# Attention values of a Flamingo-style block: split-precision matmuls into one strip, or plain float32 matmuls into four column quadrants

## The chip, the core and the metric
The kernel runs on one core of one Trainium2 chip. The metric is the time of the whole program on the device in microseconds (us). The kernel before takes 1038.49 us (median of 3 runs, 1037.32 to 1039.15).

## The reference
The program computes two residual blocks over x of shape (4, 512, 512): four batches of 512 tokens with 512 features.

```python
x = x + tanh(g_xattn) * mixture(layernorm(x), token_ids, W, W, W)   # one of 4 experts per token
x = x + tanh(g_ffn)   * ffn(layernorm(x), ...)

def ffn(hidden, ...):                      # H = 16 heads, HD = 32, R = 16, F = 2048
    x = rmsnorm(hidden, ln1_w)
    q, k, v = x @ Wq.T, x @ Wk.T, x @ Wv.T               # each split into 16 heads
    scores = q @ k.T / sqrt(32), masked below the diagonal (causal)
    attn = softmax(scores) @ v, heads joined, @ Wo.T
    mod = 0.1 * tanh(attn @ A)                           # A is (512, 16)
    h = rmsnorm(hidden, ln2_w)
    gate = silu(h @ W_in.T + mod * (h @ A) @ B)
    return hidden + (gate * (h @ W_up.T)) @ W_down.T
```

Only `attn @ A`, 16 numbers a token, is wanted of the attention. The kernel therefore folds Wo and A into the values ahead of time: each head has values of 512 keys by 16, and the sum over all heads of probabilities times values is `attn @ A`.

## The kernel before, in words
A first stage works on 19 items of tokens sorted by expert; then each of the four batches has an attention stage and an MLP stage of 16 chunks. The engines run programs that are written out by hand and meet at semaphores; each engine works strictly in its own order. Nearly all products are "split": each float32 operand is held as a high part and a rest, both in the type float32r, and a product is three matmuls (high*high, rest*high, high*rest).

The attention stage of a batch takes the 16 heads one after the other in `head_step`. For one head there are four engines in a ring:

- TensorE multiplies queries by keys into banks 0, 1 and 2 (`score_rows`, line 700): four matmuls, of 512, 384, 128 and 256 columns, since causal rows need only the keys ahead of them (1280 score columns in all for 512 queries).
- VectorE (`maxima`, line 1405) adds the mask, copies the scores to SBUF and keeps each row's maximum. ScalarE (`exponentials`, line 1038) takes the exponentials and their row sums. VectorE inverts the sums (line 1411, semaphore `rr_ok`). The rows are then multiplied by the inverse: the 512-wide part on VectorE (line 1415), the 128-wide part on ScalarE (line 1045), the 256- and 384-wide parts on GpSimd (line 493).
- TensorE turns the probabilities (ten 128x128 transposes, line 734) into banks 6, 5 and 4, which hold 256, 512 and 512 columns.
- ScalarE copies each of the three banks as the high part (line 953), VectorE subtracts it from the bank to get the rest (`low`, line 1391; semaphore `pt_lo`).
- TensorE attends (`attend`, line 797): the values of a head, also split, lie side by side as [high | rest | high of the neighbour], 48 columns, and are the stationary operand; the high and the rest of the turned probabilities are the moving one. That is eight float32r matmuls of 512, 512, 384, 384, 256, 256, 128 and 128 columns, all of them into rows 0 to 47 of bank 7, which gathers all heads. GpSimd splits the values of four heads at a time (`values_of`, lines 503 and 505).

TensorE's order in the step of head n is: turn head n+1, middle scores of n+3, attend head n with the last scores of n+3 between, first scores of n+4, and then a "filling" that belongs to something else: half a query or key projection for a later group of heads (`project_part`, steps 0 to 6), a quarter of the first MLP chunk's up product (`up_part`, line 851, steps 9 to 12), or half of the low-rank product (`low_rank_part`, line 768, steps 13 and 14). GpSimd also splits the projection weights (lines 428 and 432) after heads 0, 2 and 4.

When the last head is attended, a short chain makes the modulation: copy rows 32 to 47 of bank 7 (ScalarE), add rows 0 to 15 (VectorE, line 1544), tanh (ScalarE), two products and a split (`z_ok`, `zs_ok`). TensorE meanwhile runs the first chunk's gate product and the second chunk's up product, 12 matmuls of 512 columns each, and then waits for `zs_ok` in `modulate` (line 839).

Scores and maxima of head n may be written only when head n-3 has been turned (three buffers, `NP = 3`).

## Time and profile before

| | us |
|---|---|
| median of 3 runs | 1038.49 |
| the profiled execution, time | 1034.66 |
| its span, first to last instruction | 1032.9 |
| TensorE matmul busy | 1005.7 (97%) |
| VectorE busy | 702.4 (68%) |
| ScalarE busy | 603.7 (58%) |
| GpSimd busy | 279.2 (27%) |

The busy shares are averages over three kinds of stage. In the first batch the attention runs from about 178 us (first turned probabilities) to 243.6 us; in it VectorE, ScalarE and TensorE are all close to full, while in the MLP stages TensorE alone is. The granted TensorE clock is 1.00 of full speed in every stretch that was asked for.

### The profile page before, as it was taken

How to read it: one execution, taken by the hardware profiler on the slowest of the kernel's cores; microseconds unless marked ns; L12 is line 12 of the kernel's file. 1: busy time of each engine (PE TensorE's matmuls, PEld its weight loads, DVE VectorE, ACT ScalarE, POOL GpSimd, SP SyncE). 2: the span in 40 equal slices, each digit the busy share in tenths (PEclk: the TensorE clock that was granted, in tenths of full speed). 3: DMA queues.
4: the chain of work that ended last, by engine and by line, in shares of the span. 5: the costliest groups of instructions: out<-in, count | busy, mean ns of one | idle time of the engine just before them, and what ended most of it. 6: DMA issues, size and time to landing. Idle time of an engine off the chain costs nothing.

```text
span 1032.9 us, 16779 instructions
## 1 busy us (share of the span) xinstructions
PE 1005.7 (97%) x5140; PEld 830.0 (80%) x5141; DVE 702.4 (68%) x1841; ACT 603.7 (58%) x1447; POOL 279.2 (27%) x276
## 2 busy tenths in 40 slices
PE   6999999999999999999999999999999999999998
PEld 5787888777888888778888888778888887888886
DVE  7866755996665559985665489966655599754443
ACT  4564456997444448985344379963444499843332
POOL 4536124861000117640000148600001187300000
PEclk9999999999999999999999999999999999999999
DMA  6635133344222416434332354343234254222221
GB/s 231 216 141 173 41 122 93 83 93 163 93 91 91 132 54 184 95 104 153 96 92 91 112 158 94 77 165 96 94 98 148 57 159 100 85 82 91 91 91 52
DMA packets 47073, 115.78 MB, mean 112 GB/s; under 512 B 6800, under 2 KB 6800, under 8 KB 46096
## 3 DMA queue, kind: packets, MB, share of 16 engines
q1 hardware_dynamic: 43968, 105.06, 34.1%
q0 software_dynamic: 3040, 9.96, 2.8%
q8 instruction: 28, 0.46, 0.2%
q14 instruction: 37, 0.30, 0.1%
HBM read 76.46 MB, written 13.37 MB: 87 GB/s over the span
## 4 chain that ended last, share of the span: by engine, by line
PE 87%; DVE 4%; POOL 3%; DMA 3%; issue 2%; ACT 1%; SPq 1%; DVEq 0%
PE bank L537 67%; PE bank L734 6%; PE bank L797 6%; PE bank L700 3%; DMA stack<-wr 2%; POOL big L493 2%; PE bank L839 1%; PE bank L851 1%; DVE big L1405 1%; PE bank L593 1%; PE bank L768 1%; PE bank L608 1%; PE bank L651 1%; SPq L321 1%; DVE wr L1391 0%
## 5 line engine op out<-in xcount | busy, mean ns | idle before, releaser
L537 PE MATMUL bank<-hT,wr 128*128 128x512 f32 x1488 | 358.0, 390 | 0.0
L537 PEld LDWEIGHTS bank<-hT,wr 128*128 128x128 f32 x1488 | 279.2, 188 | 60.7 <-issue 1.6
L537 PE MATMUL bank<-wr,actr 128*128 128x512 f32 (+1 forms) x1224 | 301.6, 396 | 2.3 <-DVE actr L1373 1.5
L537 PEld LDWEIGHTS bank<-wr,actr 128*128 128x128 f32 x1224 | 227.8, 189 | 50.4 <-issue 3.0
L493 POOL TENSOR_SCALAR big<-big,rr 128x256 f32<-128x256 f32 (+1 forms) x124 | 149.2, 1212 | 76.1 <-DVE rr L1411 75.7
L432 POOL TENSOR_TENSOR wqs<-wstage,wqs 128x512 fp32r<-128x512 f32 x32 | 43.3, 1362 | 436.3 <-ACT wqs L953 435.0
L1436 DVE SCALAR_TENSOR_TENSOR wr<-stream,lns,wr 128x256 fp32r<-128x256 f32 x256 | 121.7, 536 | 52.2 <-ACT wr L1065 52.2
L1038 ACT ACTIVATE big<-big,nb 128x512 f32<-128x512 f32 (+3 forms) x256 | 140.6, 560 | 9.3 <-DVE nb L1405 9.3
L1391 DVE TENSOR_TENSOR wr<-bank,wr 128x512 fp32r<-128x512 f32 (+1 forms) x224 | 125.7, 607 | 19.3 <-ACT wr L953 18.6
L953 ACT ACTIVATE wr<-bank 128x512 fp32r<-128x512 f32 (+1 forms) x224 | 110.3, 529 | 33.5 <-PE bank L537 20.8
L953 ACT ACTIVATE actr<-act_sb 128x512 fp32r<-128x512 f32 x64 | 40.4, 632 | 146.0 <-DVE act_sb L1450 146.0
L1077 ACT ACTIVATE sil<-bank 128x512 f32<-128x512 f32 x64 | 38.2, 596 | 136.1 <-PE bank L839 136.1
L1405 DVE CUSTOM_DVE_ANT_0 big<-bank,masks 128x512 f32<-128x512 f32 (+3 forms) x256 | 110.1, 485 | 3.6 <-PE bank L700 3.5
L1065 ACT ACTIVATE wr<-stream,lns 128x256 fp32r<-128x256 f32 x256 | 108.4, 495 | 0.0
L734 PE MATMUL bank<-ident,big 128*128 128x128 f32 x640 | 88.7, 278 | 8.0 <-POOL big L493 5.1
L537 PE MATMUL bank<-hT,wqs 128*128 128x512 f32 x384 | 95.9, 393 | 0.0
L734 PEld LDWEIGHTS bank<-ident,big 128*128 128x128 f32 x640 | 70.9, 140 | 30.2 <-issue 15.9
L1391 DVE TENSOR_TENSOR wr<-stream,wr 128x512 fp32r<-128x512 f32 x64 | 43.8, 689 | 71.8 <-ACT wr L953 71.7
L797 PE MATMUL bank<-wr 128*48 128x256 f32 (+3 forms) x512 | 92.1, 310 | 0.0
L537 PEld LDWEIGHTS bank<-hT,wqs 128*128 128x128 f32 x384 | 71.5, 188 | 15.0
L1450 DVE TENSOR_TENSOR act_sb<-bank,sil 128x512 f32<-128x512 f32 x64 | 44.2, 691 | 56.9 <-PE bank L537 51.4
L1391 DVE TENSOR_TENSOR actr<-act_sb,actr 128x512 fp32r<-128x512 f32 x64 | 44.3, 692 | 44.7 <-ACT actr L953 44.7
(174 smaller groups left out, 990.3 us busy)
## 6 DMA issues: line engine op xcount, KB each, us to landing
stream<-in_wmlp SPq DMA_DIRECT2D x64, 512.0 KB, 4.0
stack<-wr SPq DMA_DIRECT2D x192, 128.0 KB, 2.3
stream<-in_wmlp SPq DMA_DIRECT2D x64, 256.0 KB, 2.7
big<-in_x SPq DMA_DIRECT2D x4, 1024.0 KB
big<-y_rows SPq DMA_DIRECT2D x4, 1024.0 KB, 5.6
residual<-big SPq DMA_DIRECT2D x4, 1024.0 KB
big<-residual SPq DMA_DIRECT2D x4, 1024.0 KB, 6.5
out<-big SPq DMA_DIRECT2D x3, 1024.0 KB, 4.8
```

The costliest lines, as they stand in the source:

```text
L432: g.tensor_tensor(wqs[:, LO, which, :, :], wqk_v[:, which, :, q * P:q * P + P], wqs[:, HI, which, :, :].bitcast(F32), ALU.subtract).then_i ...
L493: g.tensor_scalar(rows, rows, rr[:, n % 2, qt:qt + 1], None, ALU.mult).then_inc(pn_pool, 1)
L537: mm = pe.matmul(dst, lhs(pl, k), rhs(pr, k), start=start and i == 0, stop=stop and i == n - 1, skip_group_check=skip)
L734: mm = pe.transpose(bank[bk][:, col + (qt - kt) * P:col + (qt - kt) * P + P], prob[n % H % NP][:, src:src + P], ident[:, :])
L797: return pe.matmul(bank[ATT][0:3 * R, kt * P:S], vst[:, q % 2, kt, at_row:at_row + 3 * R], pts[:, j % 2, part, at:at + S - kt * P], start= ...
L953: return a.activation(dst, src, ACT.Copy)
L1038: a.activation(rows, rows, ACT.Exp, bias=nb[:, par, qt:qt + 1], scale=-1.0, accum_out=rs[:, par, qt:qt + 1]).then_inc(exp_ok, 1)
L1065: ins = a.activation(dst[:, :, dt, :], raw[:, :, dt, :], ACT.Copy, scale=lns[:, 1, dt:dt + 1])
L1391: v.tensor_tensor(dst, src, high.bitcast(F32), ALU.subtract).then_inc(done, 1)
L1405: v.tensor_tensor_reduce(prob_rows(n % H, qt), bank[bk][:, col:col + P * (qt + 1)], masks[:, S - P * (qt + 1):S], -1.0, 3.0e38, ALU.add, A ...
L1436: ins = v.scalar_tensor_tensor(out=dst[:, :, dt, :], in0=raw[:, :, dt, :], scalar=lns[:, 1, dt:dt + 1], in1=high[:, :, dt, :].bitcast(F32) ...
L1450: v.tensor_tensor(act_sb[:, :], bank[UP[par]][:, :], sil[:, :], ALU.mult).then_inc(gu_ok, 1)
```

## The change
The changed kernel attends with plain float32 matmuls instead of split ones. The values stay as they are (no splitting on GpSimd, `vst` is gone). The turned probabilities are copied once from PSUM to SBUF: banks 6 and 4 by ScalarE, bank 5 by VectorE, into two sets of buffers made of tiles that are free in this stage. The stationary operand is now 32 columns wide (this head's 16 and, unused, the next head's), and the output goes to one of four "quadrants" of bank 7, rows 0-31, 32-63, 64-95 or 96-127. For heads 4 to 15 the 1280 columns of a head are cut in six pieces so that each quadrant gets 320. For heads 0 to 3 there are four pieces of 512, 384, 256 and 128 columns that rotate over the quadrants. The quadrants are added up once a batch: ScalarE copies all of bank 7 to SBUF, one plain float32 matmul with a 0/1 matrix (`gather_rows`) sums them into bank 1, and tanh reads that bank. Half of the first gate product now runs before that matmul and half behind it (`gate_part`).

The order changes as well. The step of head n on TensorE is now: all scores of n+3, the filling (from step 7 on), attend n, turn n+1, the filling (steps 0 to 6). VectorE takes the 128-wide normalisation over from ScalarE and makes the maxima of head n+3 instead of n+2.

```diff
-NORM_DVE, NORM_ACT, NORM_POOL = (3,), 0, (1, 2)
+NORM_DVE, NORM_POOL = (3, 0), (1, 2)
+PIECES = ((0, 320, 512, 1), (2, 256, 512, 3), (0, 0, 320, 0), (1, 128, 448, 2), (3, 384, 512, 1), (1, 448, 512, 3))
...
@@ GpSimd
-                        if q == 0 and j == 0:
-                            values_of(b, 0)
-                        elif j == 2 and q < NQ - 1:
-                            values_of(b, q + 1)
...
@@ TensorE
-                def attend(kt, part):
-                    _, _, at = TURNED[kt]
-                    at_row = 64 * (j // 2) + R * (j % 2)
-                    return pe.matmul(bank[ATT][0:3 * R, kt * P:S], vst[:, q % 2, kt, at_row:at_row + 3 * R],
-                                     pts[:, j % 2, part, at:at + S - kt * P], ...)
+                def attend(kt, begin, end, quadrant):
+                    bk, col, _ = TURNED[kt]
+                    wide = R * min(2, H - head)
+                    return pe.matmul(bank[ATT][32 * quadrant:32 * quadrant + wide, begin:end],
+                                     vp_rows[:, kt, R * head:R * head + wide],
+                                     turned[j % 2][bk][:, col + begin - kt * P:col + end - kt * P],
+                                     start=head == 0, stop=False, skip_group_check=True)
+                def attend_all():
...
+                    pe.wait_ge(pt_act, n * 2 + 2)
+                    pe.wait_ge(pt_dve, n + 1)
+                    if head < QUADRANTS:
+                        for kt in range(TT):
+                            mm = attend(kt, kt * P, S, (kt + head) % QUADRANTS)
+                    else:
+                        for piece in PIECES:
+                            mm = attend(*piece)
+                    mm.then_inc(pv_done, 1)
+                if head < H - 3:
+                    scores(n + 3, other, stack_loads(b, head + 3))
+                if head >= QH * 2 - 1:
+                    filling(b, head)
+                attend_all()
                 if head < H - 1:
                     wait_probs(n + 1)
                     for kt in TURN_ORDER:
                         turn_tiles(n + 1, other, kt)
+                if head < QH * 2 - 1:
                     filling(b, head)
...
-                gate_product(0)
+                gate_part(0, 0)
+                pe.wait_ge(at_low, b + 1)
+                pe.wait_ge(rows_made, 1)
+                pe.matmul(bank[SUM][0:R, :], gather_rows[:, :], ysb[:, :], start=True, stop=True).then_inc(at_sum, 1)
+                gate_part(0, 1)
@@ ScalarE
-                for i, (bk, w, at) in enumerate(TURNED_BANKS):
-                    act.wait_ge(p_turned, n * 3 + i + 1)
-                    copy(pts[:, j % 2, HI, at:at + w], bank[bk][:, 0:w]).then_inc(pt_hi, 1)
-                    if i == 0 and (q < NQ - 1 or j < QH - 1):
-                        normalise(n + 1, q * QH + j + 1)
+                act.wait_ge(p_turned, n * 3 + 1)
+                copy(turned[j % 2][6], bank[6][:, 0:256]).then_inc(pt_act, 1)
+                act.wait_ge(p_turned, n * 3 + 3)
+                copy(turned[j % 2][4], bank[4][:, :]).then_inc(pt_act, 1)
...
-                copy(att_low, bank[ATT][32:32 + R, :]).then_inc(at_low, 1)
+                copy(ysb[:, :], bank[ATT][:, :]).then_inc(at_low, 1)
@@ VectorE
-                if two_more:
-                    maxima(n + 2, j % 2)
-                for i, (bk, w, at) in enumerate(TURNED_BANKS):
-                    dve.wait_ge(pt_hi, n * 3 + i + 1)
-                    low(pts[:, j % 2, LO, at:at + w], bank[bk][:, 0:w], pts[:, j % 2, HI, at:at + w], pt_lo)
+                dve.wait_ge(p_turned, n * 3 + 2)
+                v.tensor_copy(turned[j % 2][5], bank[5][:, :]).then_inc(pt_dve, 1)
+                if head < H - 3:
+                    maxima(n + 3, (j + 1) % 2)
...
-                v.tensor_tensor(att_sum, bank[ATT][0:R, :], att_low, ALU.add).then_inc(at_sum, 1)
```

TensorE's order in one step of the first batch's attention (before: transposes are line 734, scores 700, attend 797, filling 537). Before:

```order
L734 MATMUL bank4<-ident,big 128x128 x3
L700 MATMUL bank1<-stack 128x384 [waits nb_ok]
L700 MATMUL bank1<-stack 128x128
L797 MATMUL bank7<-wr 48x256
L700 MATMUL bank2<-stack 128x256 [waits nb_ok]
L797 MATMUL bank7<-wr 48x256
L797 MATMUL bank7<-wr 48x384 x2
L797 MATMUL bank7<-wr 48x128 x2
L797 MATMUL bank7<-wr 48x512 x2
L700 MATMUL bank0<-stack 128x512 [waits nb_ok,stk1]
L537 MATMUL bank3<-hT,wqs 128x512 [waits qk_lo,wq_lo]
L537 MATMUL bank3<-hT,wqs 128x512 x5
```

TensorE, the same kind of step in the changed kernel (filling 520, scores 683, attend 782, transposes 717):

```order
L717 MATMUL bank4<-ident,big 128x128 x3
L520 MATMUL bank3<-hT,wqs 128x512 x6
L683 MATMUL bank0<-stack 128x512 [waits nb_ok,stk0]
L683 MATMUL bank1<-stack 128x384 [waits nb_ok]
L683 MATMUL bank1<-stack 128x128
L683 MATMUL bank2<-stack 128x256 [waits nb_ok]
L782 MATMUL bank7<-big 32x192 [waits pt_dve,pt_act]
L782 MATMUL bank7<-big 32x256
L782 MATMUL bank7<-big 32x320 x2
L782 MATMUL bank7<-big 32x128
L782 MATMUL bank7<-big 32x64
L717 MATMUL bank6<-ident,big 128x128 [waits pt_act,pn_pool,pn_ok]
```

The four scores now stand together and ahead of the attend, the attend stands ahead of the next head's transposes, and it is six matmuls of 32 rows instead of eight of 48; it waits for the two copies (`pt_act`, `pt_dve`).

VectorE's order in one step, before (normalise, maxima of bank 0, 1, 1, 2, then the rests of banks 6, 5, 4):

```order
L1415 TENSOR_SCALAR big<-big,rr 128x512 [waits rr_ok]
L1405 ISA big,nb<-bank0,masks 128x512 [waits s_done,p_turned]
L1405 ISA nb 128x1
L1405 ISA big,nb<-bank1,masks 128x384 [waits s_done]
L1405 ISA nb 128x1
L1405 ISA big,nb<-bank1,masks 128x128
L1405 ISA nb 128x1
L1405 ISA big,nb<-bank2,masks 128x256 [waits s_done]
L1405 ISA nb 128x1
L1391 TENSOR_TENSOR wr<-bank6,wr 128x256 [waits pt_hi]
L1391 TENSOR_TENSOR wr<-bank5,wr 128x512 [waits pt_hi]
L1391 TENSOR_TENSOR wr<-bank4,wr 128x512 [waits pt_hi]
```

VectorE in the changed kernel (a reciprocal, two normalisations, one copy, maxima):

```order
L1393 RECIPROCAL rr<-rs 128x4 [waits exp_ok]
L1397 TENSOR_SCALAR big<-big,rr 128x512 [waits rr_ok]
L1397 TENSOR_SCALAR big<-big,rr 128x128
L1411 COPY big<-bank5 128x512 [waits p_turned]
L1387 ISA big,nb<-bank0,masks 128x512 [waits s_done,p_turned]
L1387 ISA nb 128x1
L1387 ISA big,nb<-bank1,masks 128x384 [waits s_done]
L1387 ISA nb 128x1
L1387 ISA big,nb<-bank1,masks 128x128
L1387 ISA nb 128x1
L1387 ISA big,nb<-bank2,masks 128x256 [waits s_done]
L1387 ISA nb 128x1
```

Three subtractions have become one copy, one small normalisation is added, and the copy now stands ahead of the maxima.

TensorE's order at the end of the attention, before (rest of attend 15, gate product, up product, modulate 839):

```order
L797 MATMUL bank7<-wr 48x384
L797 MATMUL bank7<-wr 48x128 x2
L797 MATMUL bank7<-wr 48x512 [waits pt_lo]
L797 MATMUL bank7<-wr 48x512
L537 MATMUL bank0<-hT,wr 128x512 [waits nb_ok]
L537 MATMUL bank0<-hT,wr 128x512 x11
L537 MATMUL bank7<-hT,wr 128x512 [waits at_sum,cg_lo,cg_hi]
L537 MATMUL bank7<-hT,wr 128x512 x11
L839 MATMUL bank0<-zst,bchunk 128x512 [waits zs_ok]
```

In the changed kernel (the summing matmul is line 905):

```order
L782 MATMUL bank7<-big 16x320 x2
L782 MATMUL bank7<-big 16x128
L782 MATMUL bank7<-big 16x64
L823 MATMUL bank0<-hT,wr 128x512 [waits nb_ok]
L823 MATMUL bank0<-hT,wr 128x512 x5
L905 MATMUL bank1<-ysb,gather_rows 16x512 [waits rows_made,at_low]
L823 MATMUL bank0<-hT,wr 128x512 x6
L520 MATMUL bank7<-hT,wr 128x512 [waits cg_lo,cg_hi]
L520 MATMUL bank7<-hT,wr 128x512 x11
L828 MATMUL bank0<-zst,bchunk 128x512 [waits zs_ok]
```

The summing matmul stands in the middle of the gate product and waits for ScalarE's copy `at_low`; the up product no longer waits for `at_sum`.

## Rows read from the trace of the kernel before

**Rows 1.** The page's part 4: the chain that ended last, by line.

```profile
PE bank L537 67%; PE bank L734 6%; PE bank L797 6%; PE bank L700 3%; DMA stack<-wr 2%; POOL big L493 2%; PE bank L839 1%; PE bank L851 1%; DVE big L1405 1%; PE bank L593 1%; PE bank L768 1%; PE bank L608 1%; PE bank L651 1%; SPq L321 1%; DVE wr L1391 0%
```

**Rows 2.** Chain of waits, first batch: start us, us, what. One step, two fillings.

```profile
195.62 1.09 PE bank L734 x10
196.72 0.23 PE bank L700 x2
196.95 0.12 PE bank L797
197.07 0.12 PE bank L700
197.19 1.04 PE bank L797 x7
198.23 0.24 PE bank L700
198.47 1.41 PE bank L537 x6
...
227.75 0.70 PE bank L851 x3
...
238.54 0.91 PE bank L768 x4
```

**Rows 3.** Groups by form: line, engine, operation, names, shape, count | busy us, mean ns.

```profile
L797 PE MATMUL bank<-wr 128*48 128x512 f32 x128 | 40.5, 394 | 0.0
L797 PE MATMUL bank<-wr 128*48 128x128 f32 x128 | 18.1, 222 | 0.0
```

**Rows 4.** Line 559 (plain float32, 64 columns): durations ns min/median/max; its warm piece.

```profile
L559 PE MATMUL bank<-bd,big x32: 217/421/447, 21.1 to 33.4; 128*128 128x64 f32 x32
```
```profile
32.70 1.00 PE L559 MATMUL bank<-bd,big 128*128 128x64 f32 x8
```

**Rows 5.** Busy time by stretch: us, engines' busy (instructions), clock, DMA share, GB/s.

```profile
216.20:243.63 27.43, 26.51 (x173) 20.45 (x174) 25.90 (x79) 24.57 (x74) 14.50 (x13) 1.00 0.29 66
```

**Rows 6.** Timeline of VectorE, one late step: start us, us, engine line op.

```profile
217.16 0.17 DVE L1411 RECIPROCAL rr<-rs 128x4 f32<-128x4 f32 x1
...
217.77 0.69 DVE L1405 CUSTOM_DVE_ANT_0 big<-bank,masks 128x512 f32<-128x512 f32 x1
...
219.41 1.61 DVE L1391 TENSOR_TENSOR wr<-bank,wr 128x256 fp32r<-128x256 f32 x3
220.95 0.18 DVE L1411 RECIPROCAL rr<-rs 128x4 f32<-128x4 f32 x1
```

**Rows 7.** Timeline of ScalarE, the same step.

```profile
217.67 1.06 ACT L953 ACTIVATE wr<-bank 128x512 fp32r<-128x512 f32 x2
218.63 0.72 ACT L1038 ACTIVATE big<-big,nb 128x512 f32<-128x512 f32 x1
```

**Rows 8.** Timelines of GpSimd and TensorE, the same step.

```profile
217.43 2.44 POOL L493 TENSOR_SCALAR big<-big,rr 128x256 f32<-128x256 f32 x2 [2.16 <-DVE rr L1411]
```
```profile
220.12 1.62 PE L734 MATMUL bank<-ident,big 128*128 128x128 f32 x10 [0.39 <-POOL big L493]
```

**Rows 9.** Timeline of TensorE: attention starts and ends, first and last batch.

```profile
178.07 1.26 PE L734 MATMUL bank<-ident,big 128*128 128x128 f32 x10
...
243.63 5.61 PE L537 MATMUL bank<-hT,wr 128*128 128x512 f32 x24
...
832.18 1.26 PE L734 MATMUL bank<-ident,big 128*128 128x128 f32 x10
...
896.81 5.61 PE L537 MATMUL bank<-hT,wr 128*128 128x512 f32 x24
```

**Rows 10.** Timeline of all engines, modulation chain of the first batch.

```profile
245.40 0.63 ACT L1125 ACTIVATE ysb<-act_sb 16x512 f32<-16x512 f32 x1 [0.75 <-DVE act_sb L1544]
...
248.08 0.68 DVE L1391 TENSOR_TENSOR zst<-sil,zst 16x512 fp32r<-16x512 f32 x1 [1.34 <-ACT zst L953]
...
249.08 0.39 PE L839 MATMUL bank<-zst,bchunk 96*128 96x512 f32 x1
```

108 lines of the change are left out of this document (38 added, 70 removed).

## The prediction

> **What bounds the kernel now.** I read the chain by line first: two thirds of it are the split products of line 537, and transposes, scores and attends (lines 734, 700, 797) are another 15% [rows 1]. So TensorE sets the time, and the attention is where the change works. The chain in order of time then shows what one step costs on TensorE: transposes 1.09 us, scores 0.23 + 0.12 + 0.24 = 0.59, attend 0.12 + 1.04 = 1.16, half a projection 1.41, together 4.25 us [rows 2]. The late fillings are 0.70 (up part) and 0.91 (low rank). In these late steps TensorE would need 1.09 + 0.59 + 1.16 + 0.70 = 3.54 us, but from one reciprocal to the next there are 220.95 - 217.16 = 3.79 us, and VectorE has no gap in them [rows 6]; its busy time is 25.9 of 27.4 us in the late half of the stage [rows 5]. So steps 0 to 6 are bound by TensorE (4.25), the later ones by VectorE (3.79). From the first transposes of a batch to the end of its last attend the stage takes 243.63 - 178.07 = 65.6 us in the first and 896.81 - 832.18 = 64.6 us in the last batch [rows 9]; I use 65.1, four times.
>
> **What the change takes off VectorE, ScalarE and GpSimd.** VectorE loses three subtractions, 220.95 - 219.41 = 1.54 us a step [rows 6], and gets one copy of 512 columns (the first maxima pass over such a bank takes 0.69 at most [rows 6]) and a 128-wide multiplication, at least 0.15, at most 0.3 us (a reciprocal of four numbers is 0.17). Its step falls to 3.79 - 1.54 + 0.7 + 0.2 = 3.15 us. ScalarE loses a copy of about 0.5 us and the small normalisation. GpSimd loses the splitting of values. None of the three is then at its limit, so what can bound the late steps is a loop of latencies, not a load.
>
> **The loop.** Let T be the end of the transposes of head n-1. ScalarE copies bank 4 after a wake-up: GpSimd's end at 217.43 + 2.44 = 219.87 and TensorE's start at 220.12 show 0.25 us for a wake-up [rows 8], and two copies take 218.63 - 217.67 = 0.96, so one takes about 0.5 to 0.6 [rows 7]. That is T + 0.8. Only then does it start the exponentials of head n+1, since it works in order: 220.95 - 218.63 = 2.3 us up to the reciprocal [rows 6, 7], T + 3.1. GpSimd starts 217.43 - 217.16 = 0.27 us later and multiplies for 2.44 us [rows 6, 8], T + 5.85; wake-up 0.25 and transposes 1.0 bring the transposes of head n+1 to T + 7.1. Two steps in 7.1 us is 3.55 a step; no step can be shorter on average. The present steps of 4.25 and 3.79 don't touch it. It is what is late next when VectorE is relieved. The move of maxima to n+3 keeps them off this loop.
>
> **The attend.** This is the term that decides, and the trace shows no plain float32 matmul of this size and no matmuls in different column quadrants. What it shows: a float32r matmul of 512 columns lasts 394 ns and one of 128 columns 222 ns, (394 - 222) / 384 = 0.45 ns a column [rows 3]; eight of them with 2560 columns take 1.16 us, 0.45 ns a column [rows 2]. The plain float32 matmuls of line 559 leave two records each (16 calls, 32 records), and a record of 64 columns lasts at least 217 ns [rows 4], as long as a float32r record of 128 columns. So a plain record costs two float32r columns per column, and a plain matmul has two records: four times. 1280 columns come to 1280 x 4 x 0.417 = 2.13 us (0.417 ns being a cycle of the 2.4 GHz level) if they run one after the other, against 1.16 now. All rests on the overlap of quadrants. Three cases:
> - *All four at once*: 320 x 4 x 0.417 = 0.53 us a head, and 512 x 4 x 0.417 = 0.85 for heads 0 to 3, mean 0.61. Starts of 12 records at some 13 ns each (the 1.04 us of seven matmuls are 2304 columns or 0.96 us and seven such gaps [rows 2]) add 0.16; entering and leaving the narrow shape is not in the trace, bounded by nothing and 0.2 us each. Range 0.65 to 1.05, I take 0.9.
> - *In order*: below, 1.2 to 1.5.
> - *One after the other*: 2.13 + 0.16, 2.3.
>
> The Trainium skill (TensorEngine Tiling, "Key Properties") says that tiles work independently, and that a change of tiling mode drains the engine. The first speaks for the case of four at once, the second against the change, twice a head. No row here shows either: the 48-row attends start 0.12 us after a score matmul and before one, without a gap [rows 2], but neither needs a quadrant. The skill measures 2.38 times for three column tiles (TensorE: Matmul & The Clock Gate, "Measured speedup vs the span model"); an estimate from that page would be 2.13 / 2.38 = 0.9 us.
>
> **The end of the stage.** Attend 15 now stands behind its own copies, with nothing between: 0.8 us of wait (wake-up and bank 4's copy, as in the loop). The summing matmul is 512 columns of plain float32: 512 x 4 x 0.417 = 0.85, with two changes of shape 0.95 us a batch on the path (0.85 to 1.3). The chain behind it is covered: today tanh starts at 245.40 and the last split ends at 248.76, 3.4 us [rows 10]. In the new order the sum ends 1.36 + 0.95 = 2.3 us after the last attend, so the chain ends near 2.3 + 0.25 + 3.4 = 5.95, while TensorE reaches `modulate` after two products and the sum, 249.08 - 243.63 + 0.95 = 6.4 [rows 9, 10]. 0.45 us of slack; if it is gone, each 0.1 us costs 0.4 in all.
>
> **The sum.** Per batch with an attend of 0.9: first transposes and projection 1.09 + 1.41 = 2.5; seven steps of 1.09 + 0.59 + 0.9 + 1.41 = 3.99, 27.9; eight steps at the loop's 3.55, 28.4 (TensorE would need 3.28 with an up part); the wait 0.8 and the last attend 0.9. That is 60.5 us against 65.1, 4.6 less. The summing matmul gives back 0.95. 3.65 x 4 = 14.6 us. The expert stage and the MLP chunks have no edit but one small reduction on VectorE in the expert stage, where TensorE's line 537 runs on; nothing. The profiled execution (1034.66) would become 1020.1; the median of the runs is 3.8 us above it, so I forecast 1038.5 - 14.6 = **1024 us**. With an attend of 0.65 or 1.05 the same sum gives 1016 and 1029.
>
> **The rivals.**
> - *In-order staircase.* The two records of one matmul go to the same quadrant, one right behind the other. If records start strictly in order, the second must wait for the first, and every record behind it waits too, so that only neighbours overlap. Then the attend costs the first records of all pieces one after the other, 1280 x 2 x 0.417 = 1.07 us, and a last record of 0.05 to 0.11, plus starts and changes of shape: 1.2 to 1.5, middle 1.35. Per batch: 2.5 + 7 x 4.44 + 4 x 3.55 + 4 x (1.09 + 0.59 + 1.35 + 0.70 = 3.73) + 0.8 + 1.35 = 64.8, and 0.95 for the sum: 0.65 more than now, 2.6 us in all, **1041**. With 1.2 it is 1034, with 1.5 it is 1048; the sign turns at an attend near 1.28 us. For it: all matmul groups in the trace follow each other in order. Against it: the records don't show when the array really starts. The Trainium skill's rule for it is that matmuls start and end strictly in order (TensorE: Matmul & The Clock Gate, "The mechanism"); no row here has two matmuls for separate quadrants, so the trace neither agrees nor disagrees.
> - *No overlap* (or plain float32 in a quadrant is slower than in the full array). Attend 2.3: steps 0 to 6 take 5.39, steps 7 and 8 3.98, 9 to 12 4.68, 13 and 14 4.30 (with 0.91), the end 3.1: 78.6 + 0.95 a batch, 14.4 more, 58 in all, **1096**. For it: the full-array cost of 2.13 is the only one that rows give. Against it: outputs of 32 rows use a quarter of the array, and they are in separate rows of the bank.
> - *The gain does not arrive.* Attends run at once, but the late steps stay near 3.79 for another reason: a late stack transfer, or VectorE's maxima of n+3, which in the steps with a projection start only after the scores. 8 x 0.24 x 4 = 8 us are lost, **1032**. Against it: the scores now start two steps after their buffer is read out, later than today, so the transfers have more room.
>
> **Chances.** Four at once 0.42; staircase 0.34; no overlap 0.12; gain cut short 0.12. What a measurement can tell from no change is 0.2%, 2 us. Faster: 0.42, and 0.11 of the last case and 0.08 of the staircase (attend below 1.2); about 0.60. Within 2 us: 0.09, nearly all staircase near 1.28. Slower: the rest of the staircase 0.18, no overlap 0.12 and a little more, 0.31. The range goes from the fastest attend (0.65 us, 1016, less 2 for a loop that is a little shorter) to the slowest staircase (1048); no overlap lies outside. The forecast's own range is 1014 to 1031.
>
> **What would show it.** In the changed profile the twelve attend records of a late head should take about 0.9 us from the first start to the first transpose, with starts of different quadrants closer than a record's length; starts in pairs with 0.13 to 0.27 us between them are the staircase, a regular 2.1 us is no overlap. Steps 1 to 6 should last 4.0 us and steps 7 to 14 3.55, with TensorE idle before line 717 and GpSimd as releaser. VectorE's busy time in the stage should fall by about 0.65 us a step. The summing matmul should take 0.85 to 1.3 us and `modulate` should not wait. I am wrong if the attend is not what sets steps 1 to 6, if the late steps are not bound by the loop, or if TensorE waits longer than 0.8 us ahead of attend 15.

## The result: 1052.7 us for 1038.1, and where the profile after shows it

The changed kernel takes 1052.71 us (median of 4 runs, 1050.51 to 1053.6), the kernel before in the same session 1038.1 us (4 runs, 1037.32 to 1039.15). The ratio is 1.0143, 95% interval [1.0126, 1.0161]: slower, with the other sign than forecast and outside the range.

The profiled execution took 1053.6 us, its span is 1051.9 us, 19.0 us more than before. Taken apart by the same marks on TensorE's timeline (first transpose of a batch, end of the last attend, `modulate`):

| | before | forecast | after |
|---|---|---|---|
| first transpose of batch 0 | 178.07 | 178.07 | 178.26 |
| attention stage, four batches | 65.56, 65.35, 65.04, 64.63 | 60.5 each | 66.36, 66.43, 70.81, 65.59 |
| last attend to `modulate` | 5.45 each | 6.4 | 7.64 to 7.67 |
| `modulate` to next batch's transpose | 147.14, 147.14, 147.52 | the same | 147.14, 148.19, 147.87 |

So of the 33.6 us between forecast and result (19.0 more in place of 14.6 less) 27.2 arose in the four attention stages (269.2 us in place of 242), 5.0 in the tails (30.6 for 25.6), 1.4 in the MLPs.

The page of the kernel after, engines and the chain by line (it answers [rows 1]; line 520 is the split product, 717 the transposes, 683 the scores, 782 the attend, 1373 VectorE's `low`, 1387 the maxima, 1397 the normalisation):

```profile
PE 994.6 (95%) x5340; PEld 809.1 (77%) x5341; DVE 664.5 (63%) x1774; ACT 558.4 (53%) x1319; POOL 264.4 (25%) x244
...
PE bank L520 64%; PE bank L717 5%; DVE big L1387 3%; PE bank L782 3%; PE bank L683 3%; DVE big L1397 2%; DVE wr L1373 2%; PE bank L828 1%; ACT big L1028 1%; DMA stack<-wr 1%; PE bank L840 1%; DMA stream<-in_wmlp 1%; PE bank L576 1%; DVE wr L1419 1%; DMA big<-in_x,gidx 1%
```

TensorE does less (994.6 us busy for 1005.7) in a longer span: the time went into its waits, and three lines of VectorE now stand on the chain with 2 to 3% each (before, the maxima had 1% and `low` 0% [rows 1]). TensorE's timeline from head 4 on (start us, us, engine, line, names, shape, count, and the idle time ahead with what ended it; it answers [rows 2]):

```profile
200.11 1.63 PE L520 MATMUL bank<-hT,wqs 128*128 128x512 f32 x6 [1.03 <-DVE wr L1373]
201.58 0.80 PE L683 MATMUL bank<-stack 96*128 96x512 f32 x4
202.31 0.35 PE L782 MATMUL bank<-act_sb,big 128*32 128x192 f32 x1
202.32 0.40 PE L782 MATMUL bank<-xi,big 128*32 128x256 f32 x1
202.32 0.46 PE L782 MATMUL bank<-act_sb,big 128*32 128x320 f32 x1
202.33 0.46 PE L782 MATMUL bank<-sil,big 128*32 128x320 f32 x1
202.50 0.33 PE L782 MATMUL bank<-act_sb,big 128*32 128x192 f32 x1
...
202.99 1.31 PE L717 MATMUL bank<-ident,big 128*128 128x128 f32 x10
204.05 1.64 PE L520 MATMUL bank<-hT,wqs 128*128 128x512 f32 x6
205.53 0.80 PE L683 MATMUL bank<-stack 96*128 96x512 f32 x4
206.26 0.75 PE L782 MATMUL bank<-big 128*32 128x192 f32 x12
206.94 1.31 PE L717 MATMUL bank<-ident,big 128*128 128x128 f32 x10
209.58 1.61 PE L520 MATMUL bank<-hT,wqs 128*128 128x512 f32 x6 [1.33 <-DVE wr L1373]
```

Read the attend first: the four quadrants' first matmuls start within 0.02 us of each other (202.31 to 202.33), the next at 202.50, and the transposes follow 0.68 us after the first start. For heads 0 to 3, with up to 512 columns in a quadrant, it is 0.97. That was the disputed term; the mean over 16 heads is 0.75 to 0.8, better than the 0.9 that I took. A step without a wait is 206.94 - 202.99 = 3.95 us, forecast 3.99. But every second step has a projection that waits more than a microsecond for VectorE's line 1373. TensorE's waits in the whole span (us in total, times, longest), the same view of the kernel before under it (there line 1391 is `low`, 734 the transposes):

```profile
PE bank L520 <- DVE wr L1373: 13.6, 12, 1.3
PE bank L782 <- DVE sil L1411: 8.2, 12, 1.3
PE bank L683 <- DMA stack<-wr: 5.8, 5, 2.5
```
```profile
PE bank L734 <- POOL big L493: 5.1, 11, 0.7
PE bank L700 <- DMA stack<-wr: 1.0, 3, 0.4
```

What the projection waits for is seen on ScalarE and VectorE (the projection that follows head 2's transposes starts at 190.35, after 1.04 us of idling):

```profile
187.28 0.50 ACT L1028 ACTIVATE big<-big,nb 128x256 f32<-128x256 f32 x1
...
187.78 0.58 ACT L943 ACTIVATE wr<-bank 128x512 fp32r<-128x512 f32 x1
```
```profile
188.70 0.90 DVE L1397 TENSOR_SCALAR big<-big,rr 128x512 f32<-128x512 f32 x2
189.52 0.68 DVE L1373 TENSOR_TENSOR wr<-bank,wr 128x512 fp32r<-128x512 f32 x1
```

The split of a finished projection (two fillings) is two operations that empty the bank which the next projection writes: a copy on ScalarE (line 943, `wr<-bank`), which the program puts behind all four exponentials of the next head, and the rest on VectorE (line 1373), behind that head's normalisation. In the kernel before, the same rest, and the filling that needs it:

```profile
187.24 0.69 DVE L1391 TENSOR_TENSOR wr<-bank,wr 128x512 fp32r<-128x512 f32 x1
```
```profile
189.82 1.54 PE L537 MATMUL bank<-hT,wqs 128*128 128x512 f32 x6
```

There the rest was done at 187.93, and the filling stood behind the transposes, scores and attend of its step: 1.9 us to spare. Now it stands right behind the transposes, with 0.73 + 0.68 + 1.06 us of scores, attend and transposes since the last filling, and TensorE is there first.

The same split feeds the stack loads of the next four heads. In step 8 it stands ahead of the copy that attend 8 needs, and then the scores of head 12 wait for their load:

```profile
219.62 0.32 PE L782 MATMUL bank<-act_sb,big 128*32 128x192 f32 x1 [1.30 <-DVE sil L1411]
...
222.51 0.91 PE L683 MATMUL bank<-stack 96*128 96x512 f32 x4 [0.91 <-DMA stack<-wr]
```

In the third batch this last wait is 2.53 us, and something follows from it that I had in no forecast: TensorE's granted clock falls. The stretch behind the wait (us, busy time of PE, PEld, DVE, ACT, POOL, clock, DMA share, GB/s), and the transposes in it:

```profile
667.50:673.50 6.00, 5.92 (x28) 4.70 (x29) 3.09 (x12) 0.73 (x3) 2.43 (x2) 0.50 0.48 109
```
```profile
671.55 2.36 PE L717 MATMUL bank<-ident,big 128*128 128x128 f32 x10
```

The clock fell by the end of the wait. At 0.50, the 1.2 GHz level, the ten transposes take 2.36 us in place of 1.31. That stage is 4.4 us longer than the first two: 1.6 us of longer wait, and some 2.8 us of work at half the clock. The tail of batch 0, TensorE and then ScalarE (it answers [rows 9, 10]):

```profile
244.62 1.65 PE L823 MATMUL bank<-hT,wr 128*128 128x512 f32 x6
247.08 1.03 PE L905 MATMUL bank<-ysb,gather_rows 128*16 128x512 f32 x2 [0.81 <-ACT ysb L943]
248.04 1.65 PE L823 MATMUL bank<-hT,wr 128*128 128x512 f32 x6
```
```profile
243.80 1.14 ACT L943 ACTIVATE wr<-stream 128x512 fp32r<-128x512 f32 x2
244.96 0.59 ACT L943 ACTIVATE ysb<-bank 16x512 f32<-16x512 f32 x1
246.43 0.60 ACT L943 ACTIVATE ysb<-bank 128x512 f32<-128x512 f32 x1 [0.88 <-DVE xi L1525]
```

The summing matmul takes 248.04 - 247.08 = 0.96 us, as forecast (0.95), but it waits another 0.81 for the copy of bank 7, which stands behind the splits of two down weights (1.14) and a copy and an addition of the low-rank product. The rest of the tail's excess, 0.4 us a batch, is in the products around the sum. The chain behind the sum is covered: `modulate` waits for nothing.

### The profile page after: what moved, and what is told of

Same layout as the page of the kernel before. It is cut to its first block, busy times and chain, and to the rows that moved or that the text cites. A ratio compares the mean times of both kernels' runs of the same rounds, so it can differ in the third digit from the quotient of the medians.

```text
span 1051.9 us, 16859 instructions
## 1 busy us (share of the span) xinstructions
PE 994.6 (95%) x5340; PEld 809.1 (77%) x5341; DVE 664.5 (63%) x1774; ACT 558.4 (53%) x1319; POOL 264.4 (25%) x244
## 4 chain that ended last, share of the span: by engine, by line
PE 80%; DVE 11%; DMA 3%; ACT 2%; issue 2%; SPq 1%; POOL 0%; DVEq 0%; ACTq 0%
PE bank L520 64%; PE bank L717 5%; DVE big L1387 3%; PE bank L782 3%; PE bank L683 3%; DVE big L1397 2%; DVE wr L1373 2%; PE bank L828 1%; ACT big L1028 1%; DMA stack<-wr 1%; PE bank L840 1%; DMA stream<-in_wmlp 1%; PE bank L576 1%; DVE wr L1419 1%; DMA big<-in_x,gidx 1%
## 5 line engine op out<-in xcount | busy, mean ns | idle before, releaser
L520 PE MATMUL bank<-hT,wr 128*128 128x512 f32 x1440 | 347.3, 390 | 1.0 <-DVE bchunk L1421 1.0
L520 PEld LDWEIGHTS bank<-hT,wr 128*128 128x128 f32 x1440 | 270.2, 188 | 59.5 <-issue 2.5
L492 POOL TENSOR_SCALAR big<-big,rr 128x256 f32<-128x256 f32 (+1 forms) x124 | 151.8, 1233 | 108.2 <-DVE rr L1393 108.2
L520 PE MATMUL bank<-hT,wqs 128*128 128x512 f32 x384 | 97.9, 398 | 13.6 <-DVE wr L1373 13.6
L520 PEld LDWEIGHTS bank<-hT,wqs 128*128 128x128 f32 x384 | 69.2, 188 | 28.8 <-issue 16.1
L717 PE MATMUL bank<-ident,big 128*128 128x128 f32 x640 | 85.0, 280 | 1.6 <-issue 1.6
L683 PE MATMUL bank<-stack 96*128 96x512 f32 (+3 forms) x256 | 55.3, 336 | 6.3 <-DMA stack<-wr 5.8
L1397 DVE TENSOR_SCALAR big<-big,rr 128x512 f32<-128x512 f32 (+1 forms) x132 | 59.2, 491 | 2.3
L943 ACT ACTIVATE big<-bank 128x512 f32<-128x512 f32 (+1 forms) x68 | 33.6, 494 | 46.9 <-PE bank L717 46.9
```

The lines of the kernel that those rows point to most:

```text
L492: g.tensor_scalar(rows, rows, rr[:, n % 2, qt:qt + 1], None, ALU.mult).then_inc(pn_pool, 1)
L520: mm = pe.matmul(dst, lhs(pl, k), rhs(pr, k), start=start and i == 0, stop=stop and i == n - 1, skip_group_check=skip)
L683: mm = pe.matmul(bank[bk][:, col:col + w], stack[:, par, 0, qt * P:qt * P + P], stack[:, par, 1, 0:w], start=start, stop=True, skip_group_ ...
L717: mm = pe.transpose(bank[bk][:, col + (qt - kt) * P:col + (qt - kt) * P + P], prob[n % H % NP][:, src:src + P], ident[:, :])
L943: return a.activation(dst, src, ACT.Copy)
L1397: ins = v.tensor_scalar(rows, rows, rr[:, par, qt:qt + 1], None, ALU.mult)
```

## The experiments

My theory after the result: the attend is as fast as hoped, and the loss is the place of the projection split in the orders of ScalarE and VectorE. Rivals: the quadrants cost more than their records show; TensorE's new order in the step, with the maxima one head further ahead, is the loss by itself; the tail. Ratios are to the kernel before, run on the same chip.

**The attend by itself: all pieces into one quadrant, and four unequal pieces.** The first (shortened; `start` and `gather_rows` follow, so that one quadrant is begun and read):

```diff
-                            mm = attend(kt, kt * P, S, (kt + head) % QUADRANTS)
+                            mm = attend(kt, kt * P, S, 0)
...
-                            mm = attend(*piece)
+                            mm = attend(*piece[0:3], 0)
```

> The changed kernel with all pieces of all heads in quadrant 0, so that no two of them can overlap (the sum then takes quadrant 0 alone); same instructions, sizes and waits otherwise. Theory 'four at once': the 0.67 us of an attend are the overlap of four quadrants; in one quadrant it takes 1280 x 4 x 0.417 = 2.13 us or a little more, TensorE bound in every step but those with slack, +1.2 to 1.45 us a step, ratio 1.07 to 1.09. Rival 'plain records are cheap': if a plain float32 record of 32 rows is simply fast, the attend stays below 1 us and the ratio near 1.014.

1113.63 us (4 runs), ratio 1.0747 [1.0727, 1.0768]. Twelve records of a late head, with the next transpose:

```profile
232.55 2.35 PE L782 MATMUL bank<-big 128*32 128x192 f32 x12
234.83 1.31 PE L717 MATMUL bank<-ident,big 128*128 128x128 f32 x10
```

2.28 us one after the other (the 2.13 + 0.16 of the prediction's third case), 0.68 in four quadrants: 3.35 times. Heads 4 to 15 in four unequal pieces, as heads 0 to 3 have them (the edit is `if head < QUADRANTS:` made `if True:`; it was tried on the mended kernel below, 1035.6 us):

> e4_split_mid with the four pieces of 512, 384, 256 and 128 columns, rotating over the quadrants, for all heads instead of the first four. Theory 'the longest quadrant sets the attend': an attend takes 0.98 us instead of 0.68 in heads 4 to 15. Only steps 4 to 6 and the last attend are bound by TensorE alone, about 0.3 x 4 us a batch, 5 us in all, ratio about 1.005; late steps stay at 3.47 us on average. Rival 'TensorE bounds all steps': 0.3 x 12 x 4 = 14 us, ratio 1.013.

1039.02 us (7 runs), ratio 1.0030 [1.0019, 1.0041], 3.4 us more than with 320 columns in each. All attends now take 0.95 to 0.98 us: an attend lasts as long as its fullest quadrant. The total is near the expected 5 us by luck. The stages grew by 7.5 us (257.0 for 249.5), since steps 9 to 14 too went from a mean of 3.48 to 3.58, and the tails and MLPs gave 3.1 back, which was no part of the expectation. The first kernel leaves no room for a staircase: 0.68 us is the overlap of all four. What a change of shape costs neither of them tells, since both change shape as often as the changed kernel.

**The projection split moved.** ScalarE splits between the second and third exponential, VectorE subtracts ahead of the normalisation:

```diff
             def exponentials(n, head, between=None):
                 for i, qt in enumerate((3, 2, 0, 1)):
+                    if i == 2 and between:
+                        between()                      # split_qk(b, *COPY_AT[q, j])
...
             def head_step(b, q, j):                    # VectorE
+                if (q, j) in COPY_AT:
+                    qk_low(b, *COPY_AT[q, j])
                 if head < H - 1:
                     normalise(n + 1, (j + 1) % 2)
...
-                if (q, j) in COPY_AT:
-                    qk_low(b, *COPY_AT[q, j])
```

> The changed kernel with the split of a query or key projection put between the second and third exponential of the same step on ScalarE, and its rest ahead of the normalisation on VectorE. Theory 'queued behind': the projections wait for this split, which is queued behind the whole set of exponentials; it comes about 1 us earlier, the waits of 1.0 to 1.3 us shrink to 0.5 or less, but the third and fourth exponentials come 0.5 us later: ratio 1.008 to 1.012. Rival 'the loop is what bounds': the delayed exponentials cost as much as the projections gain, ratio 1.014 or more.

1035.63 us (10 runs), ratio 0.9995 [0.9983, 1.0006]: more than I expected, and the whole loss. The stages are 62.75, 62.08, 62.75 and 61.96 us, 19.7 less than in the changed kernel, the span 1032.9. Its waits:

```profile
PE bank L520 <- DVE wr L1377: 1.2, 4, 0.3
...
PE bank L683 <- DMA stack<-wr: 0.9, 2, 0.5
```

The two waits fall from 13.6 and 5.8 us to 1.2 and 0.9, 17.3 us less; and the third stage, no longer behind a wait of 2.5 us, runs at a granted clock of 1.00. The cause is shown: one edit of order, no operation more or less, takes it away. My expectation counted only the first of the two waits. From here on this is the mended kernel.

**The order of TensorE and the maxima.** The step order of the kernel before (turn, then middle scores, attend, first scores, filling) with the new attend, and VectorE's maxima of n+2 behind the copy, on the changed kernel:

```diff
-                if head < H - 3:
-                    scores(n + 3, other, stack_loads(b, head + 3))
-                attend_all()
                 if head < H - 1:
                     wait_probs(n + 1)
                     for kt in TURN_ORDER:
                         turn_tiles(n + 1, other, kt)
+                ...                                     # scores 2, 0 of n+3
+                attend_all()
+                ...                                     # score 1 of n+3, score 3 of n+4, filling
```

> The changed kernel with the order of the kernel before in a step: turn n+1, middle scores of n+3, attend n, last scores of n+3, first scores of n+4, filling; maxima of n+2. The attend stays plain float32 in four quadrants, the copies stay single. Theory 'the order costs it': in the changed kernel the projections come only one attend and one set of transposes after the one whose bank they reuse, and wait 1.0 to 1.3 us three times a batch, head 12's stack loads come late; with the old order these waits go and steps 1 to 6 last about 3.8 us instead of 4.7, the late ones 3.6. The stage falls from 66.4 to about 60 us, the ratio to about 0.99. Rival 'the attend costs it': narrow matmuls slow down or drain what stands beside them; then steps 1 to 6 stay at 4.5 us or more with either order and the ratio stays above 1.005.

1082.2 us (4 runs), ratio 1.0445 [1.0427, 1.0462]; my expectation missed by more than 5%. Its waits:

```profile
ACT big L1033 <- DVE nb L1392: 90.8, 64, 1.7
...
DVE rr L1398 <- ACT big L1033: 74.3, 56, 1.3
```

ScalarE waits for every head's maxima, and VectorE then for its exponentials: the two engines take turns, a ring of 4.7 to 5.3 us a step; TensorE idles up to 1.9 us a step for it, and its granted clock is 0.50 for some 3.3 us in every stage. I then put the maxima of n+2 where they cover VectorE's wait, inside the normalisation (between the wide and the narrow multiplication), with the down weights' splits earlier as below; the projection split stays where the changed kernel has it:

> TensorE's step order of the kernel before with the quadrant attend, but VectorE makes the maxima of n+2 right behind the wide multiplication and before the copy of bank 5 (in e2_old_order they stood behind it); down splits as in e5_mid_tail. Theory 'ring of VectorE and ScalarE': e2_old_order was slow because the maxima of n+2 release the next exponentials, whose end releases the next reciprocal: 0.2 + 0.9 + 0.7 + 0.7 + 2.3 = 4.7 us a step, 5.3 with a projection's split. With the maxima moved up the ring is about 3.7 us, TensorE's own work (3.8 to 4.1 us) bounds steps 0 to 6, and the stage takes 60 to 63 us: ratio 0.990 to 0.997. Rival 'this order itself makes waits round the narrow attend': the stage stays over 66 us, ratio above 1.01.

1061.06 us (5 runs), ratio 1.0249 [1.0231, 1.0268]. Missed again. TensorE waits for the projection split here as well (15.3 us, longest 1.6), and the maxima wait for scores:

```profile
DVE big L1393 <- PE bank L683: 40.8, 70, 2.9
```

The new step order and the maxima one head further ahead are thus not the loss: both kernels that take them back are slower than the changed one. That is as far as it goes. Neither kernel tells the order from the maxima, and the old order together with the moved split was not run, so it is open whether the old order is the worse one for this attend.

**The tail.** First on the changed kernel: ScalarE takes the low-rank copy and bank 7's copy ahead of the down weights' splits, VectorE the addition ahead of its rests.

```diff
-                for par in range(2):
-                    down_high(b, par, par)
                 act.wait_ge(ha_done, b + 1)
                 ...
                 copy(ysb[:, :], bank[ATT][:, :]).then_inc(at_low, 1)
+                for par in range(2):
+                    down_high(b, par, par)
```

> The changed kernel with one order changed at the end of the attention: the low-rank copy, its sum and the copy of bank 7 stand ahead of the two splits of the down weights on ScalarE and VectorE. Theory 'queued behind': the summing matmul idles 0.81 us for a copy that is itself queued behind the weight splits and the low-rank sum, so attend end to modulate falls from 7.65 to about 6.85 us in each batch, and the ratio to the kernel before falls from 1.014 to about 1.011. Rival 'the matmul itself': the step is longer only because the plain float32 sum and its change of shape cost 2.2 us; then nothing moves (1.014).

1051.48 us (4 runs), ratio 1.0134 [1.0112, 1.0156], which can't be told from 1.0143. The tail is 6.78 us as expected, 0.87 less, but the MLPs are 148.65, 149.10 and 148.52. Then on the mended kernel, with the splits ahead of head 15's copies:

> The kernel with the split between the exponentials, and besides the two splits of the down weights moved ahead of head 15's copies, into the 1.7 to 1.9 us in which ScalarE and VectorE wait for its transposes. In e1_tail the end of the stage was 0.85 us shorter but the MLP stage behind it about 1 us longer. Theory 'late down loads': the down weights' loads of the third chunk wait for these splits, and e1_tail moved them back; here they come earlier, so attend end to modulate is about 6.8 us and the MLP stage stays at 147.5 to 148: 0.85 x 4 = 3.4 us less than e4_split_mid, ratio about 0.996. Rival 'whatever is taken off the tail comes back in the MLP stage': ratio 0.999 to 1.000.

1034.98 us (12 runs), ratio 0.9986 [0.9978, 0.9995]. Again the tail falls to 6.79 and the MLPs grow to 148.46, 149.04 and 148.36. From the last attend to the next batch's first transpose it is 155.2 to 155.9 us in both, and 155.5 to 155.8 in the mended kernel without the edit. A second limit stood behind the first.

**Copies one step earlier.** What is left in the mended stage: step 0 of 5.50 us and the 1.30 of attend 8.

```diff
-COPY_AT = {(0, 2): (2, 0), (1, 0): (2, 1), (1, 2): (3, 0), (2, 0): (3, 1)}
+COPY_AT = {(0, 2): (2, 0), (1, 0): (2, 1), (1, 2): (3, 0), (1, 3): (3, 1)}
...
                 if head == 0:
                     maxima(n + 2, 0)                   # now ahead of normalise(n + 1)
```

> The kernel with the splits in the middle of the exponentials and the down weights early, with two places of step 0 and step 8 changed: the split of the last projected K half (q 3, which 1) one step earlier (step 7 in place of step 8, its projection ends with step 6), and in step 0 the maxima of head 2 ahead of the normalisation of head 1 in place of behind it. In the kernel without this, attend 8 waits 1.30 us for the copy of bank 5, which stands behind that split's rest (0.68) and the normalisation on VectorE, and step 0 takes 5.50 us where step 1 takes 4.25. Theory (what is left of the stage is the order on VectorE alone): step 8 from 4.19 to 3.3 and step 0 from 5.50 to 4.6 to 4.9, so 1.5 to 1.8 us a batch, some 6 us in all, ratio to the kernel before 0.992 to 0.994. Rival (VectorE and ScalarE are full in these steps, so the work only comes late one step on): step 7 grows by 0.6 to 0.9, step 0 stays within 0.2, ratio 0.998 to 0.999.

1046.09 us (5 runs), ratio 1.0100 [1.0085, 1.0116]: wrong, by a third way. Step 7 takes 7.05 to 7.32 us, for 3.95. ScalarE and TensorE there:

```profile
213.26 0.60 ACT L943 ACTIVATE wr<-bank 128x512 fp32r<-128x512 f32 x1 [3.99 <-PE bank L520]
```
```profile
216.62 0.74 PE L782 MATMUL bank<-big 128*32 128x192 f32 x12 [2.76 <-DVE big L1419]
```

The projection half ends late in step 6's filling; ScalarE has begun head 8's exponentials by then and stands still among them. A split may not be asked for before its matmuls are due. Behind the wait of 2.76 us the granted clock is 0.50 for some 3.2 us in three of the four batches, as behind the late stack load above. Step 0 gained 0.2 us a batch by its own edit, which is kept below.

**What takes the tail's gain back.** I left the quadrant sum out of the mended kernel: no copy of bank 7, no summing matmul, tanh reads rows 0 to 15 of the bank (and the second up product, which overwrites that bank, waits for it).

```diff
-                copy(ysb[:, :], bank[ATT][:, :]).then_inc(at_low, 1)
-                act.wait_ge(at_sum, b + 1)
-                a.activation(att_low, bank[SUM][0:R, :], ACT.Tanh).then_inc(mod_ok, 1)
+                a.activation(att_low, bank[ATT][0:R, :], ACT.Tanh).then_inc(mod_ok, 1)
```

> The kernel with the splits in the middle of the exponentials and the down weights early, without the summing of the four quadrants: no copy of the attention's bank, no summing matmul; the tanh reads rows 0 to 15 of the bank, so three quadrants' share of the attention is left out of the modulation. Theory (the summing matmul costs its own 0.96 us on TensorE and the chain behind it is covered by the products): attend's end to modulate from 6.79 to 5.8 us, 3.8 us in all, ratio to the kernel before 0.9950. Rival (what the tail gives is taken back in the MLP, as the earlier down weights were: MLP +0.7 to +1.0): ratio 0.998 to 0.999. A third way, if the chain over the tanh had set the modulate: gap below 5.5.

1035.01 us (10 runs), ratio 0.9991 [0.9980, 1.0002]: nothing, though the tail falls to 5.56 to 5.60 us. The MLPs are 149.63, 152.06 and 151.42. ScalarE and TensorE at chunk 2 of the second batch, SyncE's queue ahead of it, and the stretch by two microseconds (us, busy time of PE, PEld, DVE, ACT, POOL, clock, DMA share, GB/s):

```profile
470.02 1.71 ACT L1053 ACTIVATE wr<-stream,lns 128x256 fp32r<-128x256 f32 x4 [3.23 <-DMA stream<-in_wmlp]
```
```profile
473.87 4.60 PE L520 MATMUL bank<-hT,wr 128*128 128x512 f32 x12 [3.27 <-DVE bchunk L1425]
```
```profile
458.98 0.37 SPq L293 DMA_DIRECT2D big<-y_rows  x1
459.39 1.29 SPq L327 DMA_DIRECT2D big<-in_x  x1
461.03 0.96 SPq L299 DMA_DIRECT2D stream<-in_wmlp  x1
```
```profile
464.00:466.00 2.00, 2.00 (x11) 1.63 (x10) 0.56 (x1) 0.60 (x1) 0.00 (x0) 1.00 1.05 409
```

Chunk 2's weights come behind 2 MB of the next batch's y and x on a path that moves some 400 GB/s, and all of it is issued when the stage ends. The first batch's MLP grew by 1.2 us, just the tail's gain. The other two grew by 3.0: 1.4 us of longer waits, and the clock again. Behind the waits of 3.27 and 1.81 us the granted clock is 0.50, and 12 matmuls take 4.60 us, where they take 3.02 in the first batch. So I put the weights of chunks 2 and 3 first, on the mended kernel with the sum (besides it has step 0's edit):

```diff
+                for par in range(2):
+                    load_chunk(b, 2 + par, par)
                 if more:
                     load_y(b + 1)
                     load_x(b + 1)
-                with sp.Fori(1, NCH // 2) as c2:
+                with sp.Fori(2, NCH // 2) as c2:
```

> The kernel with the splits in the middle of the exponentials and the down weights early, with SyncE's loads at the end of the stage in another order: the MLP weights of chunks 2 and 3 (1.5 MB) ahead of the next batch's y and x (2 MB) in place of behind them, and in step 0 the maxima of head 2 ahead of the normalisation of head 1. The trace of that kernel without this has 2 MB of y and x in front of the weights; the DMA engines move some 400 GB/s there, and the first product of chunk 2 waits 0.54, 1.86 and 0.38 us in batches 0 to 2 for the weights' split, which waits for the load (0.50, 1.81, 0.27). Leaving out the quadrant sum took 1.23 us from the tail and gave it back in longer MLPs (149.6 to 152.1 for 148.4 to 149.0), with waits of 1.73, 3.27 and 1.81 there. Theory (the loads set the start of chunk 2, so what the tail gives is taken back until they come earlier): these waits go, end of attend to next turn from 155.3 to 155.8 down to some 154.6, with 0.2 a batch from step 0 about 3.5 us in all, ratio to the kernel before 0.995 to 0.9965. Rival (the y and x loads, now later by 3.8 us, hold up VectorE's first rows, or the MLP has another limit): MLP stays at 148.5 to 149, ratio 0.998 to 0.999.

1029.22 us (5 runs, 1028.87 to 1030.79), ratio 0.9935 [0.9921, 0.9948]: the fastest complete kernel of this study, and more than I expected. The medians differ by 5.8 us from the kernel without the edits, and not all of that is theirs: the profiles show 3.0 us less in the MLPs and 1.0 less in the stages, and 2.4 less ahead of the first stage, where the granted clock differed (last section). The runs with a mean granted clock of 1.000 took 1033.4 (one) and 1028.87 to 1029.22 us (three), 4.2 to 4.5 us apart. The MLPs are 147.81, 147.14 and 147.94, the waits at chunk 2 are gone: the weights are issued at 455.01 in the second batch, 2.5 us ahead of the end of its last attend, and y at 457.67. ScalarE's first split of chunk 2 in the second batch, without idle time ahead of it:

```profile
466.59 1.70 ACT L1057 ACTIVATE wr<-stream,lns 128x256 fp32r<-128x256 f32 x4
```

The same edit without the sum:

> The kernel without the quadrant sum (three quadrants' share is left out of the modulation) with the MLP weights of chunks 2 and 3 loaded ahead of y and x. Theory (loads took the tail's gain back): waits of 1.73, 3.27 and 1.81 us at chunk 2 go, end of attend to next turn from 155.2, 157.6 and 157.0 to some 153.4, and the sum's price of 1.2 us a batch shows: some 8 us less than with the loads behind, ratio to the kernel before 0.990 to 0.993. Rival (another limit in the MLP): ratio 0.998 to 0.999, as without.

1025.96 us (4 runs), ratio 0.9898 [0.9883, 0.9913]. From the last attend to the next first transpose it takes 153.44, 152.72 and 153.50 us, for 154.59, 153.94 and 154.71 with the sum: the sum costs 1.2 us a batch, as the tail had said, once the loads are out of the way. (The medians are 3.3 us apart; this kernel lacks step 0's 0.2 us a batch, and its profiled execution lost 1.3 us to the clock ahead of the first stage.) And the same edit on the kernel before:

> The kernel before, with the one edit of the loads that made the changed attend's mended version faster: weights of chunks 2 and 3 ahead of y and x on SyncE's queue. It tells how much of that version's 7 us is the new attend and how much the loads. Theory (the kernel before has no wait for these loads: its y and x are issued at 240.63 and 241.05, about 3 us before its stage ends, and its MLPs take 147.14 to 147.52 us): the same time, ratio 0.998 to 1.001. Rival (the order of the loads is worth something by itself there too): ratio 0.996 or less, and the new attend is worth that much less.

1036.88 us (12 runs), ratio 1.0007 [0.9997, 1.0016]: nothing there. The order of the loads is worth nothing by itself; it lets the new attend's gain through. The new attend with the orders that fit it is worth 0.5 to 0.8% (5.5 us between the profiled executions, 7 between the medians). The other orders, the projection split and the down weights' splits earlier and step 0's maxima, were not tried on the kernel before, so their share in this is not shown; its trace has no wait of TensorE for a projection split [rows 2].

## Why the prediction was wrong, point by point

- **What bounds the kernel.** Right for the kernel before. The reading was carried over without asking which other user of an engine's order becomes due earlier.
- **The attend.** Right mechanism (four at once, chance 0.42), 0.68 and 0.97 us where I took 0.9. The Trainium skill (TensorEngine Tiling, "Key Properties") has tiles independent, and the starts within 0.02 us agree. The same section's draining at a change of mode is hardly seen: 320 columns in two records of 2 x 0.417 ns a column are 0.53 us, and 0.68 to the next transpose leaves 0.15 for the starts and the change back; the change ahead of it can hide in the scores, which now take 0.73 us and took 0.59 [rows 2]. The staircase, which I derived from the Trainium skill's rule that matmuls start and end strictly in order (TensorE: Matmul & The Clock Gate, "The mechanism"), is not there. The pieces do start in the program's order, which agrees with the rule; but three more quadrants start while the first one's second record is still to come, so my step from the rule to the staircase was wrong. The 2.38 times that the Trainium skill measures for three column tiles (TensorE: Matmul & The Clock Gate, "Measured speedup vs the span model") has its like here in 3.35 times for four.
- **Steps 0 to 6: the step that failed.** I wrote 1.09 + 0.59 + 0.9 + 1.41 = 3.99 us, seven times. Without a wait it is 1.06 + 0.73 + 0.68 + 1.48 = 3.95. But the sum has only TensorE's own work in it. The bank of the projections has a reader on two other engines, and steps 1, 3 and 5 wait 1.0 to 1.3 us for it: 13.6 us in all. With the late stack loads (5.8) and the clock that fell behind the longest of them that is the miss's core, as the moved split showed: 19.7 us of the 27.2 in the stages. The other 7.5 are in the mended kernel too: step 0 (5.50, 4.83, 5.49, 4.71 for 3.99) is 4.6 us over, steps 1 to 6 (4.25, 4.49, 4.25, 4.19, 3.95, 4.49) are 6.7 over, by scores and projections that lie 0.14 and 0.07 above [rows 2], the attends of 0.97, and short waits in steps 2, 4 and 6; what follows is 3.7 under.
- **Steps 7 to 14.** The loop of 3.55 us is right: in the mended kernel steps 9 to 14 alternate between 3.28 and 3.66, in the changed one 3.23 to 3.73, but for the third batch's step 10 (4.31, at the low clock) and the waits at steps 8 and 9. In the mended kernel heads 9 to 14 are turned 0.10 us after GpSimd's end, here 228.89 + 2.44 = 231.33 and 231.43:

```profile
228.89 2.44 POOL L492 TENSOR_SCALAR big<-big,rr 128x256 f32<-128x256 f32 x2 [1.22 <-DVE rr L1397]
```
```profile
231.43 1.28 PE L717 MATMUL bank<-ident,big 128*128 128x128 f32 x10 [0.20 <-issue]
```

  From one head's transposes to those of the second next it is 231.43 - 224.49 = 6.94 us; I had derived 7.1. The margin is small: TensorE alone needs 3.28 a step. I had a late stack transfer among the rivals and argued that it had more room. It had less: with the split that feeds it moved ahead, its wait falls from 5.8 to 0.9 us.
- **VectorE's relief.** Forecast 0.65 us a step; 702.4 - 664.5 = 37.9 us over 64 heads is 0.59. Right. Steps 9 to 14, which took 3.54 to 4.62 us in the first batch before, are down to 3.48 on average in the mended kernel. In steps 0 to 6 the relief bought nothing: the engine's order, not its load, was the limit.
- **The last wait.** 0.69 us for 0.8. Right.
- **The tail.** The matmul was right (0.96), `modulate` doesn't wait; the 0.81 us for the copy of bank 7 was left out. I counted the chain behind the sum and not the one ahead of it: 3.2 of the 5.0 us. The rest is 0.4 us a batch in the 24 products, which take 5.83 us around the sum (6.79 - 0.96) and 5.56 to 5.60 without it.
- **No edit in the MLP, so nothing there.** Half right in the changed kernel (1.4 us), and misleading beyond it: `load_y` now waits for the attends (`pv_done`) and not the transposes (`p_turned`), so y is issued 0.2 us after the stage's end and not 3.0 us ahead of it. It is one line of the full change, and I gave it no line. No run puts the old wait back by itself.
- **The rivals.** None of them was the one that came; the late stack transfer in the last of them was a part, priced at 8 us less gain together with the maxima and never as a loss. The slower side of the range rested on the attend alone, and the clock was in no rival.

What stays open: step 0's remaining 1.3 us, and attend 8's wait of 1.30, which no version here removed at a gain.

## What to carry to other kernels

When a step gets shorter, list every buffer that is written once a step or every second one, and for each what its readers stand behind on their own engines; the engine that got faster meets the one whose reader is queued last. An expected gain that shows in its own stretch but not in the total may have been taken back by the next limit, here a 2 MB load in front of the one that was needed: look at what the moment that came earlier still has to wait for. Sum the waits ahead of a new instruction as well as those behind it. And read the granted clock behind every long wait of TensorE: the wait's price can be more than its length.

## What the runs showed of the hardware

- Plain float32 matmuls with 32-row outputs in four column quadrants run at once: 2.28 us in one quadrant, 0.68 in four with 320 columns each, 0.97 with up to 512.
- A wait of TensorE can take its granted clock from 1.00 to 0.50. It did so behind waits of 2.53 us (changed kernel), 2.76 us (three times of four, copies one step earlier), 3.27 and 1.81 us (no sum), and not behind 1.73 us (no sum, first batch) or 1.86 us (down splits earlier, second batch). At 0.50 ten transposes took 2.36 us for 1.31, and 12 matmuls of 512 columns 4.60 for 3.02.
- The first 60 us are not alike in all executions. The stretch from 20 to 40 us of the mended kernel with earlier down splits, and below it the same of the fastest one (columns as above; the last but two is the granted clock):

```profile
20.00:40.00 20.00, 16.44 (x62) 13.93 (x63) 15.37 (x43) 8.95 (x15) 14.15 (x15) 0.87 0.82 285
```
```profile
20.00:40.00 20.00, 16.16 (x69) 13.81 (x70) 15.52 (x44) 8.95 (x15) 14.50 (x15) 1.00 0.82 284
```

  With a granted clock of 0.87 there (0.96 in the next 20 us) the first attention stage begins at 180.84 us, with 1.00 at 178.49. A span of one profile can so carry 2 us that have nothing to do with the edit. The stages' own lengths are the better measure, as long as the granted clock within them is 1.00.
